# Graph layer on one core: 332 edge groups instead of 336, a shorter softmax prelude, and sums handed over by halves in the message stage

## The reference, cut to what matters

```
score = s_src[src] + s_dst[dst] + diff . a_dif + |diff| . a_abs + (hr_src * hr_dst) . a_prd      # diff = hr_dst - hr_src, per head
alpha = leaky_relu(score, 0.2)
att   = softmax of alpha over the edges with the same src
out[src] += att * h_e[dst]
```

## Time and profile before

| | us |
|---|---|
| runs, median (lowest to highest) | 3062.76 (3058.04 to 3062.81) |
| the profiled execution, its own time | 3091.47 |
| its span, first to last instruction | 3089.7 |
| PE busy | 2429.0 (79%) |
| DVE busy | 1674.3 (54%) |
| POOL busy | 1538.7 (50%) |
| ACT busy | 1051.7 (34%) |
| mean granted clock of PE | 0.914 |

### The profile page before, as it was taken

One profiled execution on the slowest core, in us unless ns is written; L12 is line 12 of the kernel. 1 busy time (PEld: TensorE's weight loads), 2 busy tenths in 40 slices (PEclk: granted clock), 3 DMA queues, 4 the chain that ended last, 5 costly groups with the idle time before them and its releaser, 6 DMA issues. The chain is left out here.

```text
span 3089.7 us, 46311 instructions
## 1 busy us (share of the span) xinstructions
PE 2429.0 (79%) x13776; PEld 1711.6 (55%) x13776; DVE 1674.3 (54%) x2574; ACT 1051.7 (34%) x2469; POOL 1538.7 (50%) x1567
## 2 busy tenths in 40 slices
PE   3999968989998898998940577777777777667898
PEld 3565646666666666666620455555555555555343
DVE  7677634444444444444479566666666566566222
ACT  1333323334343343433320333333333333333221
POOL 2233255555555555556510556666665666541244
PEclk7999989999999999999975798999998999888899
DMA  4111166676676766667650566666666666565343
GB/s 147 43 53 54 46 174 189 185 191 185 188 186 190 192 183 190 188 185 187 189 189 36 179 170 174 178 176 179 173 177 174 178 181 175 164 162 222 95 127 96
DMA packets 178642, 490.49 MB, mean 159 GB/s; under 512 B 40386, under 2 KB 58722, under 8 KB 176366
## 3 DMA queue, kind: packets, MB, share of 16 engines
q0 software_dynamic: 117200, 387.44, 45.7%
q1 hardware_dynamic: 46918, 74.05, 7.6%
q10 hardware_dynamic: 14296, 26.03, 2.7%
HBM read 441.16 MB, written 48.17 MB: 158 GB/s over the span
## 5 line engine op out<-in xcount | busy, mean ns | idle before, releaser
L1377 PE MATMUL ps_sum<-messages,node_onehot 128*125 128x260 f32 x2688 | 715.3, 421 | 273.6 <-ACT node_onehot L1464 99.0
L993 POOL DMA_INDIRECT rows_v<-target_rows,edge_dst x672 | 684.6, 1019 | 487.9 <-ACT edge_terms L1080 271.5
L1285 POOL DMA_INDIRECT rows_e<-message_rows,edge_dst x672 | 640.2, 953 | 561.0 <-DVE messages L1299 206.1
L1377 PEld LDWEIGHTS ps_sum<-messages,node_onehot 128*125 128x125 f32 x2688 | 537.1, 207 | 455.8 <-issue 189.5
L1034 PE MATMUL ps_w<-source_onehot_t,edge_space 125*128 125x256 bf16 x4032 | 529.2, 278 | 71.8 <-issue 71.1
L1073 ACT ACTIVATE w_abs<-ps_w 128x1024 f32<-128x1024 f32 x336 | 344.4, 1027 | 633.9 <-remote 339.1
L1034 PEld LDWEIGHTS ps_w<-source_onehot_t,edge_space 125*128 x4032 | 397.8, 99 | 152.1 <-issue 102.7
L1013 DVE SCALAR_TENSOR_TENSOR w_abs<-w_abs,corner 128x512 f32<-128x512 f32 x672 | 459.5, 745 | 20.8 <-ACT w_abs L1073 20.7
L1308 DVE TENSOR_TENSOR edge_space<-ps_sum,edge_space 125x520 f32 x336 | 234.5, 698 | 406.0 <-PE ps_sum L1377 211.6
L1029 PE MATMUL ps_w<-ident,rows_v 128*128 128x128 f32 x2688 | 378.2, 283 | 58.5 <-issue 39.1
L1006 DVE TENSOR_SCALAR source_onehot_t<-edge_ids,iota_col 125x512 bf16<-125x512 bf16 x168 | 64.1, 382 | 655.6 <-remote 372.5
(11 more groups left out here) (385 smaller groups left out, 2217.2 us busy)
## 6 DMA issues: line engine op xcount, KB each, us to landing
edge_ids<-local_ids ACTq DMA_DIRECT2D x84, 250.0 KB
rows_v<-target_rows,edge_dst POOLq DMA_INDIRECT x672
scores<-score SPq DMA_DIRECT2D x672, 16.0 KB
rows_e<-message_rows,edge_dst POOLq DMA_INDIRECT x672
up_t<-in_up_dram SPq DMA_DIRECT2D x4, 2048.0 KB, 17.0
scores<-score SPq DMA_DIRECT2D x336, 8.0 KB
from_right<-scores SPq DMA_DIRECT2D x2, 2688.0 KB, 12.3
edge_space<-scores SPq DMA_DIRECT2D x2, 2688.0 KB, 23.9
```

The costliest lines, as they stand in the source:

```text
L993: nc.gpsimd.indirect_dma_start(rows[q][:, j, :], None, tab_v, bass.IndirectOffsetOnAxis(ap=edge["dst"][:, tile:tile + 1], axis=0)).then_in ...
L1285: nc.gpsimd.indirect_dma_start(rows[q][:, j, :], None, tab_e, bass.IndirectOffsetOnAxis(ap=edge["dst"][:, tile:tile + 1], axis=0)).then_in ...
L1377: ins = nc.tensor.matmul(ps_sum[q % SUMS][:, half, 0:HALF], onehot[q % MARKS][:, j, :], messages[q % BUFS][:, j, half * HALF:(half + 1) * ...
```

## The change

- `in_turns` and the loops of the score and message stages stop after 332 groups. SP stores zeros as the scores of the last four groups. The bookkeeping of score stores follows (the last set has four groups instead of eight).
- The store of the sort's result writes sources instead of records, so the softmax needs no shift. The two scans become two comparisons with the piece's first and last source. DVE no longer clears the sums: ACT does it in two copies, the first 5376 columns after DVE has used `from_left`, which lies there, and the rest at once. The load of the third score part waits for the second.
- Score stage: DVE's list becomes multiply(n-5), locate(n); seven source one-hots.
- Message stage: PE computes one half of the columns (260) after the other and signals each; DVE adds each half by itself, and two groups behind; six node one-hots.

```diff
-    groups = turns * bufs
+    groups = min(turns * bufs, MAX_GROUPS)
...
# score_edges
-    PAIRS, MARKS, TURNED, SET = 3, 5, 3, P // (GROUP * HEADS)
+    PAIRS, MARKS, TURNED, SET = 3, 7, 3, P // (GROUP * HEADS)
...
+            for g in range(MAX_GROUPS, GROUPS):
+                sp.wait_ge(zeros_set, 1)
+                sp.dma_start(scores[:, g * GE:(g + 1) * GE], zero_scores[:, :]).then_inc(zeros_out, 16)
-            for n in range(GROUPS // 2):
+            for n in range(MAX_GROUPS // 2):
...
-            in_turns(TURNS, ((0, locate), (7, multiply)), TURN)
+            in_turns(TURNS, ((5, multiply), (0, locate)), TURN)
...
# softmax_weights
             for k, part in enumerate(score_parts):
+                if k == 2:
+                    sp.wait_ge(scores_in[1], 16)
...
-            link(v.tensor_scalar(keys[:, :], keys[:, :], KEY.bit_length() - 1, None, ALU.logical_shift_right))
+            v.tensor_copy(end_keys[:, 0:1], own[:, 0:1])
+            v.tensor_copy(end_keys[:, 1:2], own[:, PIECE - 1:PIECE])
             link(v.tensor_tensor(reset[:, :], keys[:, 1:PIECE + 2], keys[:, 0:PIECE + 1], ALU.not_equal))
             link(v.tensor_scalar(reset[:, :], reset[:, :], -BIG, None, ALU.mult))
-            v.tensor_tensor_scan(in_first, reset[:, 0:PIECE], floor, 0.0, ALU.add, ALU.max)
-            link(v.tensor_tensor_scan(in_last[:, ::-1], reset[:, 1:PIECE + 1][:, ::-1], floor, 0.0, ALU.add, ALU.max))
+            v.tensor_scalar(in_last[:, :], own, end_keys[:, 1:2], -BIG, ALU.not_equal, ALU.mult)
+            link(v.tensor_scalar(in_first, own, end_keys[:, 0:1], -BIG, ALU.not_equal, ALU.mult))
...
-            v.memset(sums[:, :, :], 0.0)
...
+            act.wait_ge(nothing_set, 1)
+            nc.scalar.copy(flat_sums[:, PIECE:size], nothing[0:L, 0:1].broadcast_to([L, size - PIECE]))
+            act.wait_ge(left_used, 1)
+            nc.scalar.copy(flat_sums[:, 0:PIECE], nothing[0:L, 0:1].broadcast_to([L, PIECE]))
...
# gather_messages
-    BUFS, SUMS, RING, TURN, MARKS, LAID = 3, 2, 6, 12, 4, 28
+    BUFS, SUMS, RING, TURN, MARKS, LAID, HALVES = 3, 2, 6, 12, 6, 28, 2
...
-                at_least(dve, summed, n + 1)
-                at_least(dve, added, n)
-                total = sums[:, DS(b, 1), :].rearrange("p o (i x) -> p (o i) x", i=2)
-                v.tensor_tensor(total, ps_sum[q % SUMS][:, :, 0:HALF], total, ALU.add).then_inc(added, 1)
+                for half in range(HALVES):
+                    at_least(dve, summed, n * HALVES + half + 1)
+                    at_least(dve, added, (n - 1) * HALVES + half + 1)
+                    total = sums[:, DS(b, 1), half * HALF:(half + 1) * HALF].rearrange("p o x -> p (o x)")
+                    v.tensor_tensor(total, ps_sum[q % SUMS][:, half, 0:HALF], total, ALU.add).then_inc(added, 1)
...
-            in_turns(TURNS, ((0, weigh), (1, add_up), (1, mix_step)), TURN)
+            in_turns(TURNS, ((0, weigh), (2, add_up), (1, mix_step)), TURN)
...
-                at_least(pe, added, n - SUMS + 1)
-                for j in range(GROUP):
-                    for half in range(2):
+                for half in range(HALVES):
+                    at_least(pe, added, (n - SUMS) * HALVES + half + 1)
+                    for j in range(GROUP):
                         ins = nc.tensor.matmul(ps_sum[q % SUMS][:, half, 0:HALF], onehot[q % MARKS][:, j, :], messages[q % BUFS][:, j, half * HALF:(half + 1) * HALF],
                                                start=j == 0, stop=j == GROUP - 1)
-                ins.then_inc(summed, 1)
+                    ins.then_inc(summed, 1)
```

More of the change, by code:

```diff
@@ L305, in _ @@
             g_.iota(head_i[:, :], pattern=[[1, 1]], base=0, channel_multiplier=1).then_inc(iotas_ready, 1)
-            g_.memset(ends[:, :], PAD_RECORD).then_inc(ends_set, 1)
+            g_.memset(ends[:, :], KEY - 1).then_inc(ends_set, 1)
             g_.memset(row_e[:, :, :], 1.0).then_inc(row_ones_set, 1)
@@ L931, in score_edges @@
         ps_heads = [ps(f"ps_heads{h}", [P, 512]) for h in range(2)]
+        zero_scores = sb("zero_scores", [(KF + 1) * HEADS, GE])
+        zeros_set, zeros_out = sem("zeros_set"), sem("zeros_out")
         located = sem("located")
@@ L945, in use_of, with ends_set @@
             return pair + pair // SET_PAIRS
+        LAST, SETS = MAX_GROUPS - 1, -(-MAX_GROUPS // SET)
+        USES = MAX_GROUPS // 2 + SETS
         def use_of_terms(k):
-            return k * (SET_PAIRS + 1) + SET_PAIRS
+            return min(k * (SET_PAIRS + 1) + SET_PAIRS, USES - 1)
         def stores_before(use):
-            return sum(HEADS if u % (SET_PAIRS + 1) == SET_PAIRS else KF for u in range(use % BUFS, use, BUFS))
-        USES = use_of_terms(GROUPS // SET - 1) + 1
+            return sum(HEADS if u % (SET_PAIRS + 1) == SET_PAIRS or u == USES - 1 else KF for u in range(use % BUFS, use, BUFS))
+        def ends_set(n):
+            return n % SET == SET - 1 or n == LAST
         block = ctx.enter_context(nc.Block())
@@ L973, in _ @@
                                  score[u % BUFS][c * STRIP:c * STRIP + HEADS, :]).then_inc(score_out[u % BUFS], 16)
-                if n % SET_PAIRS == SET_PAIRS - 1:
+                if ends_set(2 * n + 1):
                     k = n // SET_PAIRS
                     u = use_of_terms(k)
+                    size = min(SET, MAX_GROUPS - k * SET)
                     sp.wait_ge(score_kept, u + 1)
                     for h in range(HEADS):
-                        sp.dma_start(scores[KF * HEADS + h, k * SET * GE:(k + 1) * SET * GE].rearrange("(t e) -> t e", e=P),
-                                     score[u % BUFS][h * SET * GROUP:(h + 1) * SET * GROUP, 0:P]).then_inc(score_out[u % BUFS], 16)
+                        sp.dma_start(scores[KF * HEADS + h, k * SET * GE:(k * SET + size) * GE].rearrange("(t e) -> t e", e=P),
+                                     score[u % BUFS][h * SET * GROUP:(h * SET + size) * GROUP, 0:P]).then_inc(score_out[u % BUFS], 16)
             for u in range(USES, USES + BUFS):
                 sp.wait_ge(score_out[u % BUFS], 16 * stores_before(u))
+            sp.wait_ge(zeros_out, 16 * (GROUPS - MAX_GROUPS))
         @block.gpsimd
         def _(pool):
-            for n in range(GROUPS):
+            for n in range(MAX_GROUPS):
                 q = n % RING
@@ L998, in _ @@
             v = nc.vector
+            v.memset(zero_scores[:, :], 0.0).then_inc(zeros_set, 1)
             def locate(n, q, turn):
@@ L1111, in softmax_weights @@
         alpha, from_right, in_last = sb("alpha", [P, PIECE]), sb("from_right", [P, PIECE]), sb("in_last", [P, PIECE], BF16)
-        in_first = keys[:, 0:PIECE].bitcast(F32)
-        lowest = sb("lowest", [P, 1])
+        own = keys[:, 1:PIECE + 1]
+        in_first = own.bitcast(F32)
+        end_keys, nothing = sb("end_keys", [P, 2]), sb("nothing", [P, 1])
         score_parts = (alpha[:, :], from_right[:, :], from_left, weights.rearrange("p c i h -> p (c i h)"))
```

25 lines of the change are left out of this document (14 added, 11 removed).

## The result

The changed kernel took 3036.84 us (median of 5 runs, 3029.24 to 3043.70), the kernel before 3062.76 (3058.04 to 3066.80; the table above has the first three of its five runs). The ratio is 0.9918, 95% interval 0.9896 to 0.9941. The forecast was 2900, range 2830 to 3005: wrong in size, right in sign. Its profiled execution took 3036.84 us (span 3035.0); the one of before had 3091.5, 29 us above its median, so a difference of the two spans shows 54.7 us where the medians show 25.9.

A forecast was written before the change was run, and what follows sets the result against it. It took PE to be nearly full in the scores, and no engine full in the messages, where pauses cost time. Savings 14.0 + 17 + 12.5 + 120 = 163.5 us from 3062.8 gave 2900, range 2830 to 3005.

The forecast's parts named there:

- Softmax, -17: Softmax: dropped shift and scans, score loads in sequence, and clearing moved to ACT save 17 us, bounds 4 and 24.
- Four groups: Scores and messages: 332 of 336 groups run, saving 14.0 and 12.5 us.
- New order in the scores, 0: Scores: multiply before locate and seven source one-hots remove DVE's waiting but gain 0 us, bounds -4 and +4.
- the 20 that the prediction named as its end: Scores: the prediction called itself wrong if this stage gained more than 20 us.
- messages, -120 (and -12.5): Messages: additions by halves, two groups behind, and six one-hots save 120 us; four groups fewer save 12.5 more.
- 1.4 us saved: Messages, after each pause: PE waits for half an addition, about 0.42 us and 0.1 more, in place of 1.95.
- I count 50 pauses: Messages: 44 unnamed DVE waits and a few that fell while DVE was busy; saving 70 us in all.
- between pauses: Messages: 236 groups outside pauses run at PE's 1.75 us instead of 2.0; 59 us, taken as 50.
- B: Rival, messages hardly gain: pauses are PE's own, ACT's one-hots set the time after; 2989, or 3019 with none; chance 0.19.
- C: Rival, messages slower: PE's pauses come with its signals, so twice the signals double them; 3164 us; chance 0.09.
- A: Rival, messages: POOL becomes the bound at 2.51 us a group; 2821 us, half-way forms 2840 to 2870; chance 0.18 with these.
- wrong if the messages take over 980 us: Messages: the prediction's sign of being wrong; it expected this stage near 920 us.

The follow-up runs named there:

- job 3: Chip with late signals: changed kernel 3068.1 us, with message edit undone 3062.2; without message gathers after the sixth group 2695.5 and 2808.1.
- job 1: Changed kernel, chip with late signals: one signal a group 3085.0 us; additions one group behind 3064.1; whole sums two behind 3065.4; message edit undone 3060.2.
- job 2: Chip without late signals: changed kernel without most message gathers 2490.6 us, message edit also undone 2605.0; kernel before with 332 groups ratio 0.9916, plus softmax 0.9848.

## Why the prediction was wrong

**Where it held.** *Softmax, -17*: 108.7 us from its first load to the next stage, 126.5 before, so -17.8; 17.2 and 19.6 in the paired runs on chips without late signals. The steps came as worked out (start us, length us, changed kernel):

```profile
1575.01 0.14 DVE L1178 CAST ends<-in_last 128x1 f32<-128x1 bf16 x1
1576.85 5.76 DVE L1182 TENSOR_TENSOR alpha<-alpha,from_right 128x5376 f32<-128x5376 f32 x1 [1.69 <-DMA from_right<-scores]
1585.90 5.76 DVE L1182 TENSOR_TENSOR alpha<-alpha,edge_space 128x5376 f32<-128x5376 f32 x1 [3.29 <-DMA edge_space<-scores]
1592.31 5.76 DVE L1182 TENSOR_TENSOR alpha<-alpha,edge_space 128x5376 f32<-128x5376 f32 x1 [0.65 <-DMA edge_space<-scores]
1598.66 5.76 DVE L1186 TENSOR_TENSOR alpha<-alpha,from_right 128x5376 f32<-128x5376 f32 x1 [0.60 <-DMA from_right<-scores]
```

From the stage's first instruction at 1561.4 the additions start 15.4, 24.5, 30.9 and 37.3 us later; forecast from the data loads were 15.5, 24.7, 31.1 and 37.5. VectorE waits for a DMA before each: the stage's head is now bound by 13 MB of loads. ScalarE's last copies end it:

```profile
1639.10 4.67 ACT L1215 COPY edge_space<-nothing 125x5376 f32<-125x5376 f32 x1 [73.20 <-DVEq L1194]
...
1667.73 2.05 ACT L1223 COPY edge_space<-ps_weight_t 128x128 f32<-128x128 f32 x10 [1.21 <-PE ps_weight_t L1233]
```

*Four groups*: 21.4 and 21.1 us on chips without late signals, which is four groups at the pace there, 4 x (955.4 + 831) / 332 = 21.5. The method was right; 26.5 was its value at the first chip's pace. *New order in the scores, 0*: 955.4 us with either order on one chip.

**Where it is not settled.** On chips with late signals the message edit undone leaves 27 to 28 us of gain for groups, softmax and score order, and 43.5 were forecast; the intervals reach from 17 to 39 us. The two first traces show 25.1 us off the scores, over the 20 that the prediction named as its end, but the same code, 1139.9 us in that execution, took 1153 to 1160 in eight later ones on such chips: it was a difference between executions or chips. Whether the groups or the new order in the scores are worth less there was not found out.

**The step that failed: messages, -120 (and -12.5).** The part reads: after a pause VectorE "has two groups' messages ready", "1.4 us saved", "I count 50 pauses", so 70 us, and "between pauses" 50 more. The second term came in part (other stands 52 us less between the first two traces, 24 less in job 3). The first did not: instead of 70 us less, the stands with a late signal took 26 us more between the first two traces and 36 more in job 3, and slow matmuls 32 and 26 more. The step that failed is what a pause was taken for: one late signal of a fixed length, 5.2 us in the row it was read from, behind which only VectorE's 1.95 us could change. The traces show three things of a pause.

*Its length is not fixed.* The longest lateness in a cluster (the start of an addition that had to wait, less the end of its group's or half's last matmul record) averages 4.2 us before and 6.6 in the changed kernel; in job 3 it is 4.4 with the message edit undone and 6.4 with it. That is 2.0 to 2.4 us more, where the edit was to save 1.4. In job 1 it is 4.1 undone, 4.9 one group behind, 5.2 with whole sums two behind and 6.4 with one signal. Why it grows when TensorE has more in store was not found out; a part may be that an earlier group is then caught by the same pause.

*The signals come late, and many of them at once.* The prediction read it so ("then both come at once"), and the trace of before has it (with the earlier trace rows):

```profile
2011.91 0.38 PE L1385 MATMUL ps_mix<-ident,kt_in 128*125 128x128 f32 x2
...
2013.90 0.37 ACT L1475 COPY k_rows<-ps_mix 125x256 f32<-125x256 f32 x1 [4.78 <-remote]
```

VectorE is released at 2013.87 for the group of 2006.68 and ScalarE 0.03 us later for two matmuls that TensorE has behind the whole next group (2010.09, eight matmuls, 1.99 us). By the semaphore updates kept in the traces, 138 of the 541 recorded signals of the messages' matmuls in the changed kernel come within 0.5 us of the one before, 153 of 549 on the second chip and 19 of 270 before; on chips without late signals none does, and halves are at least 0.8 us apart. In the scores 46 to 63 do on chips with late signals, 0.19 us apart at the least, where a chip without has at least 2.19. So TensorE had gone on with its work during part of the pause. Inside a pause there are single signals too: of additions whose matmuls were both issued before the first of them was released, and for both of which VectorE waited over 0.15 us, 222 of 233 in three traces (changed kernel on two chips, one group behind on one) are a multiple of 0.713 us apart, from 1 to 12 of them, to within 0.08 us, where 22% would be by chance. A choice of pairs that both waited leaves the bursts out.

*For another part TensorE stops.* In the scores it stops inside a run of twelve matmuls that wait for nothing (message edit undone, job 1; then 332 groups and softmax, job 2, where the same run is whole):

```profile
609.25 0.54 PE L1048 MATMUL ps_w<-source_onehot_t,edge_space 125*128 125x256 bf16 x2
610.23 0.39 PE L1048 MATMUL ps_w<-source_onehot_t,edge_space 125*128 125x256 bf16 x2 [0.45 <-issue]
611.67 1.03 PE L1048 MATMUL ps_w<-source_onehot_t,edge_space 125*128 125x256 bf16 x8 [1.05 <-issue]
...
611.78 1.02 ACT L1087 ACTIVATE w_abs<-ps_w 128x1024 f32<-128x1024 f32 x1 [5.50 <-remote]
```

```profile
605.62 1.48 PE L1048 MATMUL ps_w<-source_onehot_t,edge_space 125*128 125x256 bf16 x12
```

The last two pieces start 1.44 us apart, twice 0.72. TensorE's gaps are 1.5 us here, while ScalarE stands 5.5 us for a signal that is 4.6 us late (its matmuls' records end at 607.18). How much of the lateness is such a stop can be bounded in the scores, where TensorE is busy 955 of 955 us on a chip without late signals and has nothing to catch up with: a chip with them loses 202 us (1157 - 955), clock included, while ScalarE's waits of over 0.9 us beyond TensorE's records come to 386 us, 128 of them, in the trace whose two stages are shown under job 3. So there about half of the lateness is lost by TensorE at the most. For the messages this was not found out: the run that asks it met no chip with late signals.

A full TensorE can hide less of it. Without gathers TensorE is busy 670.6 of 677 us in the changed order and 709.7 of 788 in the old one, which leaves it up to 78 us in which a stop costs nothing. Of the 126 us by which gathers cost the changed order more on a chip with late signals (381 against 255), that slack would be up to 72 (78 less 6), slow matmuls are 31 ((117.2 - 3.2) - (91.4 - 7.9)), and 23 are left unassigned. This is an account by sums, argued and not shown. The clock goes the same way: 0.87 for the changed kernel in job 3, 0.91 with the message edit undone.

Of the rivals B comes nearest ("the pauses are PE's own", 3019 with none of the 120; it had 0.19), 18 us under the measured time. That the pauses are TensorE's own is borne out in part only, and ScalarE's one-hots, its other cause, are not it: their waits did go. C counted right in one place (stands with a late signal 45 to 78) and wrong in cause: the clusters went from 64 to 66 with twice the signals, and one signal a group was slower still. A's floor is real, but on the other kind of chip: there POOL's 2.50 us a group bind already before the change. The prediction's own sign of being wrong ("wrong if the messages take over 980 us") came true. On both kinds of chips the edit is worth nothing or next to it, for opposite reasons; with no gathers it is worth 111 to 114 us.

By the Trainium skill, "VectorE: DVE Perf Modes", section on the TRN2 errata, the second addition pays a fixed cost again. The trace agrees (2 x 421 ns against 698). That it cost nothing follows where POOL's pace binds; with late signals VectorE waits 375 us before its additions in the changed kernel.

## What to carry to other kernels

Before pricing what follows a late signal, ask what a pause itself is: look for gaps inside runs of the engine's instructions that wait for nothing, and see by two waiting engines whether its signals come one by one or all at once. A saving per pause holds only if the change leaves the pauses' number and length alone, so compare both afterwards; here the number stayed near, as chains count it, and the length grew by more than was to be saved. Write down each engine's own floor for the stage (here POOL's 2.50 us a group) beside the mean that a disturbed trace shows, and run the unchanged kernel on a second chip before trusting a gain that is made of gaps.

## What the runs showed of the hardware

- The kernel before takes 3094 us on two chips (3063 on a third) and 2685 on three others: in the variants the score stage takes 1140 to 1160 against 955 us, the messages, in any order that was run there with all gathers, 1034 to 1059 against 829 to 833, all else within 6 us. The excess lies only in the two stages with POOL's gathers, and goes when the gathers go (677.4 and 676.8 us on one chip of each kind).
- There TensorE's signals come late, 60 to 75 times in the 1034 to 1059 us of the messages, by up to 15 us: some of them a multiple of 0.71 us apart, the rest in bursts, with 0.06 us between halves that are at least 0.8 us apart elsewhere. TensorE's own matmuls stop in between for a part of it. The granted clock of the message stage is 0.86 to 0.91, against 0.98 to 1.00 without late signals. What makes the signals late is open, as is whether it takes an indirect gather or only its traffic.
- A gather of 128 rows of 2 KB occupies POOL 0.95 us and the next starts 0.30 us later; a plain load of the same bytes takes it 0.55 us.
